# Stacked bf16 products moved onto two 64-row halves in a 1-core transformer kernel

## The reference, cut to what matters

```
x = x + 0.5 * routed_ffn(layernorm(x))          # f1
x = x + retention(layernorm(x))                 # r2: scores = (q k^T) * decay mask, no softmax
x = x + 0.5 * routed_ffn(layernorm(x))          # f3
x = x + 0.5 * relative_ffn(layernorm(x))        # f4: softmax(q k^T + q p^T shifted) v, then 32 experts
x = x + plain_attention(x)                      # a5: softmax(q k^T) v
x = x + 0.5 * relative_ffn(layernorm(x))        # f6: as f4
```

## Time and profile before

| | us |
|---|---|
| median of 3 runs | 2753.72 |
| lowest, highest | 2753.01, 2758.3 |
| span of the profiled execution | 2756.7 |

### The profile page before, as it was taken

One profiled execution on the slowest core, in us unless ns is written; L12 is line 12 of the kernel. 1 busy time (PEld: TensorE's weight loads), 2 busy tenths in 40 slices (PEclk: granted clock), 3 DMA queues, 4 the chain that ended last, 5 costly groups with the idle time before them and its releaser, 6 DMA issues. The chain is left out here.

```text
span 2756.7 us, 60632 instructions
## 1 busy us (share of the span) xinstructions
PE 2491.5 (90%) x19804; PEld 1926.5 (70%) x19804; DVE 1958.6 (71%) x4716; ACT 1626.3 (59%) x4737; POOL 1666.1 (60%) x2470
## 2 busy tenths in 40 slices
PE   7999699799969999999977988998899999997898
PEld 5788567578858877777777445665787777776743
DVE  5554488455548999999954566775789999996545
ACT  3333244233329888888842335777798888885222
POOL 4322666333226688888842764553668888884366
PEclk9999899899979999999989998999999999998999
DMA  3810366460012222222335236553222222242622
GB/s 120 322 66 1 83 142 139 148 257 1 1 33 47 49 62 62 61 63 60 102 95 160 52 76 137 108 116 69 47 47 61 62 61 53 50 122 65 181 62 68
DMA packets 231992, 242.00 MB, mean 88 GB/s; under 512 B 27538, under 2 KB 203922, under 8 KB 224498
## 3 DMA queue, kind: packets, MB, share of 16 engines
q1 hardware_dynamic: 182530, 196.14, 27.6%
q0 software_dynamic: 12288, 25.19, 3.4%
q10 hardware_dynamic: 36864, 16.79, 2.1%
HBM read 99.28 MB, written 134.41 MB: 85 GB/s over the span
## 5 line engine op out<-in xcount | busy, mean ns | idle before, releaser
L2804 ACT ACTIVATE f4a_pr<-f4a_sr,f4a_nm 128x256 f32<-128x256 f32 x512 | 238.9, 479 | 52.1 <-DVE f4a_nm L2870 51.8
L2804 ACT ACTIVATE f6a_pr<-f6a_sr,f6a_nm 128x256 f32<-128x256 f32 x512 | 238.8, 479 | 50.1 <-DVE f6a_nm L2870 49.7
L3007 POOL TENSOR_TENSOR f4a_rr<-a5b_room 128x256 f32<-128x256 f32 x256 | 195.7, 765 | 81.1 <-DVE a5b_room L2878 74.0
L3007 POOL TENSOR_TENSOR f6a_rr<-a5b_room 128x256 f32<-128x256 f32 x256 | 195.4, 763 | 74.2 <-DVE a5b_room L2878 67.5
L2006 DVE TENSOR_REDUCE a_nm<-a_sr 128x2 f32<-128x512 f32 x256 | 166.8, 684 | 69.8 <-PE a_sr L1739 68.8
L2878 DVE TENSOR_TENSOR a5b_room<-f4a_ur,f4a_turn 128x512 f32<-128x512 f32 x256 | 174.0, 680 | 32.7 <-PE f4a_ur L2664 30.9
L2878 DVE TENSOR_TENSOR a5b_room<-f6a_ur,f6l_turn 128x512 f32<-128x512 f32 x256 | 174.0, 680 | 27.1 <-PE f6a_ur L2664 25.4
L2679 PE MATMUL f6a_sr<-f6l_pe_hi,f6a_rr_hi 128*128 128x256 f32 x512 | 187.7, 367 | 0.0
L2679 PE MATMUL f4a_sr<-f4a_pe_hi,f4a_rr_hi 128*128 128x256 f32 x512 | 187.7, 367 | 0.0
L2870 DVE TENSOR_REDUCE f4a_nm<-f4a_sr 128x2 f32<-128x512 f32 x256 | 174.6, 682 | 18.1 <-PE f4a_sr L2681 17.8
L2870 DVE TENSOR_REDUCE f6a_nm<-f6a_sr 128x2 f32<-128x512 f32 x256 | 174.5, 682 | 17.3 <-PE f6a_sr L2681 16.9
(11 more groups left out here) (634 smaller groups left out, 8261.1 us busy)
## 6 DMA issues: line engine op xcount, KB each, us to landing
slots<-f_zero SPq DMA_DIRECT2D x100, 512.0 KB
f4m_xr<-slots SPq DMA_DIRECT2D x128, 64.0 KB, 2.2
slots<-f4m_y ACTq DMA_DIRECT2D x128, 64.0 KB, 2.2
f6m_xr<-slots SPq DMA_DIRECT2D x128, 64.0 KB, 2.2
slots<-f6m_y ACTq DMA_DIRECT2D x128, 64.0 KB, 2.3
r_scratch<-r_parts SPq DMA_DIRECT2D x32, 192.0 KB, 2.3
all_qs<-r_scratch SPq DMA_DIRECT2D x16, 384.0 KB, 4.9
all_ks<-r_scratch SPq DMA_DIRECT2D x16, 384.0 KB, 6.8
```

Source lines behind the costliest of these rows:

```text
L2804: last = nc.scalar.activation(pr[:, n % 4, x, :], sr.bank(b, n)[:, x * T:(x + 1) * T], ACT.Exp, bias=nm[:, n % SB, x:x + 1], accum_out=zs[ ...
L3007: nc.gpsimd.tensor_tensor(rr[:, hs % RAW, :], tmp[:, hs % 2, 0, :], tmp[:, hs % 2, 1, :], ALU.add)\
```

## The change

- Every stacked tile has 128 partitions and 8 head places: heads of one half of the array's rows on partitions 0 to 47, the other eight on 64 to 111 (`rows(g)`). A content, score or turned matmul has 48 rows (60 in the turned ones, with 12 rows for maxima) from partition 0 or 64. No zero rows are kept, and their memsets go (in the routed layers and at the start of the plain attention).
- Plain attention: scores of slot n lie on one half, the turned product of the same slot on the other. They are issued alternately: score 0, turned 0, score 1, turned 1, and the projection comes behind them. The maxima travel in two transfers per half.
- Relative attention: content and `relate` matmuls are issued alternately, with `AHEAD` = 6 so that they lie on different halves; the position matmuls follow; `small` comes behind them.
- Retention: the four heads of a group lie on one half; the order of issue is as before.
- Relative attention and the head start of f6 inside a5: the remainder is taken from the bank by VectorE (n = 11; in a5 this was GpSimd), and the fp32 copy `qk` goes. The residual's sum of n = 7 moves to n = 6.
- SP reads a batch with four transfers instead of two.

```diff
-ROWS = 96
-KROWS = ROWS + 3 * H // 2
+HS = H // 2
+TILE = 64
+USED = SLOTS * HD
+TOP = 3 * QUAD
...
+def rows(g, first=0, number=USED):
+    return slice(g * TILE + first, g * TILE + first + number)
+
+
+def read_slots(sp, tiles, scratch, stacked):
+
+    for u, dst in enumerate(tiles):
+        slots = scratch[u].rearrange("n (d g h) t -> g (n d) (h t)", g=2, h=HS)
+        for g in range(2):
+            sp.dma_start(dst[rows(g), :, :].rearrange("s h t -> s (h t)"), slots[g]).then_inc(stacked, 16)
...
+                own = rows(r % 2)
                 for j in range(QUAD):
-                    h = j * QUAD + r
-                    mm = nc.tensor.matmul(sd[:, n % DB, j, :], ks[0:ROWS, par, h, block_], qs[0:ROWS, par, h, block_], start=True,
-                                          stop=True)
+                    h = r // 2 * QUAD + j
+                    mm = nc.tensor.matmul(sd[:, n % DB, j, :], ks[own, par, h, block_], qs[own, par, h, block_], start=True, stop=True)
...
-                    if s == G + 2:
-                        nc.vector.memset(stack[0][32:64, :], 0.0)
...
     def take_heads(self, act, i, bank):
-        if i:
-            act.wait_ge(self.rest1, i)
         if i >= 2:
             act.wait_ge(self.bounced, (i - 1) * BOUNCED)
-        self.nc.scalar.activation(self.qk[:, :, :].rearrange("p u t -> p (u t)"), bank, ACT.Copy)
-        return self.nc.scalar.activation(self.parts[:, i % 2, 0, :, :], bank.rearrange("p (u t) -> p u t", u=2), ACT.Copy)
+        self.nc.scalar.activation(self.parts[:, i % 2, 0, :, :], bank.rearrange("p (u t) -> p u t", u=2), ACT.Copy)\
+            .then_inc(self.part1, 1)
...
+    def rest_of_heads(self, dve, i, bank):
+        dve.wait_ge(self.part1, i + 1)
+        if i:
+            dve.wait_ge(self.parts_ready, i)
+        return self.nc.vector.tensor_tensor(self.rest[:, :, :], bank.rearrange("p (u t) -> p u t", u=2),
+                                            self.parts[:, i % 2, 0, :, :], ALU.subtract)
...
+            def products(it, n):
+                (b, hs), i = relating(it, n), attend(it)
                 if b is not None:
-                    relate(b, hs)
+                    relate_room(b, hs)
+                if i:
+                    pe.wait_ge(sr.emptied, sr.nth(i, n))
+                for x in range(2):
+                    if i:
+                        contents(i, n, x)
+                    if b is not None:
+                        relate(b, hs, x)
+                if i:
+                    positions(i, n)
...
                 for n in range(NR):
+                    products(it, n)
                     small(it, n)
-                    related(it, n)
-                    if attend(it):
-                        scores(attend(it), n)
```

More of the change, by code:

```diff
@@ L935, in heads_of @@
     return at(*v)
-STACKED = 16 * 2 * len(RUNS)
+STACKED = 16 * 2 * 2 * len(RUNS)
 def slots_of(part, run, each, n):
-    return bass.AP(part.tensor, part.offset, [[each, run], [H * n, HD], [1, H * n]])
-USED = 6 * HD
-BOUNCED, LANDED = 16 * 6, 16 * 2
+    return [bass.AP(part.tensor, part.offset + g * HS * n, [[each, run], [H * n, HD], [1, HS * n]]) for g in range(2)]
+BOUNCED, LANDED = 16 * 6, 16 * 4
+def rows(g, first=0, number=USED):
[5 more added lines that the diff above has]
+            sp.dma_start(dst[rows(g), :, :].rearrange("s h t -> s (h t)"), slots[g]).then_inc(stacked, 16)
 def write_slots(sp, parts, scratch, bounced):
@@ L1670, in at, with late @@
             return i if i is not None and i >= first else None
+        def late(s, n):
+            m = (n - TURNED) % NS
+            return at(s, n, TURNED + m), m
         def ahead(s, n, slot, of=2):
@@ L1857, in _ @@
                 for n in range(NS):
-                    i = batch(s, 2)
+                    i, (e, m) = batch(s, 2), late(s, n)
                     if i is not None:
-                        scores(i, n)
+                        scores_room(i, n)
+                    if e is not None:
+                        turned_room(e, m)
+                    for x in range(2):
+                        if i is not None:
+                            scores(i, n, x)
+                        if e is not None:
+                            turned(e, m, x)
                     project(s, n)
-                    for m in range(NS):
-                        i = at(s, n, TURNED + m)
-                        if i is not None:
-                            turned(i, m)
                     for r in range(QUAD):
@@ L1905, in small @@
                             act.wait_ge(moved[half], i * MOVED)
-                        copy(mrow[0:TOP, half, :], desk.bank(f"m{half}", i)[0:TOP, 0:T]).then_inc(desk_taken, 1)
+                        copy(mrow[0:2 * TOP, half, :], desk.bank(f"m{half}", i)[0:2 * TOP, 0:T]).then_inc(desk_taken, 1)
                 i = at(s, n, 5, MADE)
@@ L2040, in small @@
                     lead.measure_tokens(dve, i)
+                i = ahead(s, n, 15)
+                if i is not None:
+                    lead.rest_of_heads(dve, i, desk.bank("lqk", i)).then_inc(lead.rest1, 1)
                 i = ahead(s, n, 8, 1)
@@ L2077, in split_maxima @@
                 whole = nm[:, half, :, :]
-                first, second, third = (mf[:, half, :, n * HALF:(n + 1) * HALF] for n in range(3))
+                first, second, third = (mf[:, half, :, 0:2 * TOP].rearrange("p t (g n j) -> p n t g j", g=2, n=3)[:, n] for n in range(3))
+                by_tile = "p t (g j) -> p t g j"
+                whole4, r4, b4 = [v.rearrange(by_tile, g=2) for v in (whole, r1[:, :, :], b2[:, :, :])]
                 nc.gpsimd.tensor_copy(b1[:, :, :], whole).then_inc(split, 1)
@@ L2769, in _ @@
             pe.wait_ge(k.loaded, k.loaded_count)
-            run(step, related)
+            run(step, products)
         def take_turned(eng, b, n, copy):
```

211 lines of the change are left out of this document (92 added, 119 removed).

## The result

| | before | after |
|---|---|---|
| median, us (5 runs each) | 2753.72 (2748.25 to 2758.3) | 2799.6 (2792.62 to 2814.28) |
| ratio of the two, 95% interval | 1 | 1.0165 (1.0147 to 1.0184) |
| span of the profiled execution, us | 2756.7 | 2812.5 (its time 2814.28) |

What follows compares the result with a forecast made beforehand. TensorE was taken to bound r2 and a5, TensorE and VectorE equally f4 and f6. Relative attentions -22, a5 -10, r2 +17, the rest -0.4 sum to -15.4 us: median 2738, own range 2722 to 2752.

Steps and rivals of the forecast that it cites:

- Pairs side by side: f4, f6, a5: paired matmuls on different row halves run together, gaining 0.19 us per slot, 3.0 us a batch.
- The pairs don't overlap: Rival, attentions: the 3.0 us gain per batch is missing, +114 us, 2868 us; chance 0.07.
- Division by rows is free: Rival: changing to row halves costs nothing; f4 and f6 -67, a5 -25, r2 0, 2662 us; chance 0.13.
- Entry 0.10: TensorE, r2 and attentions: changing into the row halves costs 0.10 us each time, with bf16 weights.
- Leaving 0.16: TensorE, r2 and attentions: returning from row halves to full width costs 0.16 us each time, with fp32 weights.
- Full price at the exit: Rival: leaving the halves costs 0.25 us, as fp32 weights can't load ahead; +47 us, 2800 us; chance 0.20.
- my 1.1: r2: new mode changes around projections between scores add 1.1 us a batch, +17 us in all.
- a5's waits: a5: TensorE's waits grow from 0.8 to 1.2 us a batch, as VectorE needs 0.68 us per slot's maxima.
- The remainder: f4, f6: read from the bank it takes 0.69 us instead of 1.70, so VectorE loses 1.0 us a batch.
- The desk's waits: f4, f6: of 1.3 us a batch that TensorE waits for xt and rz, 1.0 goes with the new order.
- The waits only change hands: Rival, f4 and f6: desk time spared returns as waits for x2t or VectorE; 2760 or 2752 us; chance 0.18.
- The zero fills: f1 and f3: a VectorE zero fill of 1.76 us before the last sum goes, saving 0.2 us each.

Runs made afterwards that it cites:

- mix_r2_96rows: Changed kernel with r2's scores back on 96 rows (48 of them zeros, filled by GpSimd at r2's start), f4, a5 and f6 on two halves: 2777.67 us, ratio 1.0082.
- changed_again: The changed kernel itself, unaltered, timed once more beside the kernel before on another chip: 2835.94 us, ratio 1.0168.
- mix_r2_old: Changed kernel with r2's old tiles, reads and order of heads, but its scores still reading 48 rows: 2803.59 us, ratio 1.0180.
- r2_rows48: Kernel before, with only r2's two score matmuls reading rows 0 to 48 in place of 0 to 96: 2785.28 us, ratio 1.0107.
- r2_tiny_mode: Kernel before, r2's scores on 96 rows, one added 48-row, one-column matmul ahead of each of six projections a batch: 2771.34 us, ratio 1.0054.

## Why the prediction was wrong

Two steps failed: the clock, which the sum put at nothing, and TensorE's waits in the relative and plain attentions, which I let shrink or hardly grow. A third term, the price of leaving the halves, was mis-sized.

- **Pairs side by side: right.** 0.21 us a slot against the 0.19 that I took. *The pairs don't overlap* and *Division by rows is free* are out.
- **Entry 0.10: right** (0.096). **Leaving 0.16: too low.** It is 0.19 where fp32 weights follow, past the 0.18 from which I let *Full price at the exit* decide; on my own count of 680 exits the 0.03 are 20 us, which alone turn 2738 into 2758. That this rival said 2800 and the kernel takes 2799.6 is luck: its exit of 0.25 is not there, and it holds nothing of the clock. In r2 the modes cost 0.83 us a batch, less than my 1.1.
- **The clock: the step that I did not take.** I worked every stage at the upper level because the earlier trace rows showed it there. r2 and a5, whose scores now read 48 rows, got stretches at the lower level. In the profile of after r2's +47 is 13 for the modes and, by difference, 34 for the clock. mix_r2_96rows shows that all of it goes with the 48 rows. No run put 96 rows back in a5, so there it is only likely. In a5, by the scores' starts, nine batches are 17.2 us in place of 16.0, 11 more, and the last but one 22.1 in place of 19.4; the second is 16.2 in place of 21.7, which takes 5.5 back. In f4 and f6 the 48-row matmuls brought no falls in the steady part (1.00 from 940 to 1370 us).
- **a5's waits.** I let them grow from 0.8 to 1.2 us a batch. They are (11.2 + 9.4 + 2.4 us for ScalarE) / 190 × 17.07 = 2.1 us. The batch of 15.3 became 15.8 at the upper level.
- **The remainder: the size was right, the conclusion wrong.** 0.68 us against 0.69 forecast. But "VectorE loses 1.0 us a batch" was not so: in the later batches VectorE waits for GpSimd, and what one instruction doesn't wait another one does. That the 1.70 in the earlier trace rows was mostly waiting I had said; I did not ask who would inherit it. Nor did the shortening need the bank: with the new order alone it is 0.75 us.
- **The desk's waits went, as said (15.1 us to none), and came back at the exponentials** (9.0 to 25.0). That is *The waits only change hands*, which held in f4 and f6 with 0.3 us a batch on top; I gave it 0.18. TensorE's waits in f4 are (25.0 + 2.9) / 430 × 36.94 = 2.4 us a batch; I had 1.2, and took 0.3 off for VectorE's queue. Its own work is 36.9 − 2.4 = 34.5 us, even less than my 35.1, so the waits are the step that failed there.
- **The zero fills.** I had 0.2 us for VectorE's; with the three on GpSimd at the end of f1, r2's first instruction comes 3.9 us earlier (296.84 to 292.93) and its first score 6.3.
- **A slip in a rival's sum.** Without overlap a5 loses the 3.0 us too, so its term is 3.0 − 0.7 = 2.3 a batch and not 1.7; the rival is 2877, not 2868. Nothing else rests on it.

The 46 us of the medians are thus for the larger part r2's clock and modes. 96 rows there brought the ratio from 1.0165 to 1.0082, with 15 us of zero fill in it. How large the part is varies with the falls: r2 has 47 us of 56 in the first profile and 26 in that of changed_again, whose median is 45 us over the kernel before.

## What to carry to other kernels

Before you take rows of the array away from a stage that is bound by TensorE, ask what else keeps the granted clock up; compare the clock in a window of that stage before and after, and count a full-width projection between divided matmuls as 0.15 to 0.3 us more. When an instruction is slow because it waits for a shared port, making it independent only hands the wait to the next one: relieve the engine on the other side. A change with several parts is best timed part by part, since here the reading from the bank alone was slower, the order alone made no difference, the two together were faster, and the halves cost more than that.

## What the runs showed of the hardware

- The granted clock fell in a stage where TensorE was busy 96% of the time and never waited over 0.6 us. Its mean over 345 to 500 us was 0.86, 0.91 and 0.96 in three kernels whose scores read 48 rows (changed, mix_r2_old, r2_rows48), 0.96 with 64 rows, 0.98 with 72, and 1.00 with 96 rows though the batches were as long and had as many gaps (r2_tiny_mode). As one kernel had 0.86 and 0.96 in two profiles, this is no scale by rows. Two or three full-width matmuls more a batch held it at 1.00. The Trainium skill (TensorE: Matmul & The Clock Gate, A second HAM failure mode: psum-queue depth-cycling) tells of short idle times between groups of matmuls that make the clock swing between its levels. The swinging is here; that short gaps alone do it, r2_tiny_mode does not bear out.
- In the middle of a stage a fall lasts 3.4 or 6.8 us and comes at most once a batch, often at nearly the same place of it (447.7 and 461.4 us); at the start of r2 one lasted 44 us in the changed kernel, 7 in the kernel before.
- Changing between 64-row tiles and full width costs 0.10 us into the tiles (medians of 105 and 108 slots) and 0.19 out of them with fp32 weights behind (141 and 143 slots).
- A VectorE operation on eight columns waited for the end of GpSimd's subtraction of two SBUF tiles (1.24 us in place of 0.15), and did not wait for a GpSimd send beside it.
- Left open: which property of the divided matmuls the clock follows. Rows read and changes of mode go together at 48 and 64 rows, and 72 rows, without any change of mode, gave one fall and a ratio whose interval barely clears 1 (1.0003 to 1.0022): a hint, no more.
